# Sorted experts: the silu product kept in PSUM and split there, and the low halves of the weights shared out anew between POOL and DVE

## The reference, cut to what matters

```python
for e in range(e_tot):                                    # 9 experts, hidden width 704
    h = _silu(x_flat @ ew1[e].T) * (x_flat @ ew3[e].T)
    out = out + cw[:, e:e + 1] * (h @ ew2[e].T)            # cw: zero but for the token's two
```

## Time and profile before

| what | value |
|---|---|
| median of 3 runs | 3542.73 us |
| lowest and highest | 3534.68, 3547.43 us |
| span of the profiled execution | 3539.1 us |
| mean granted TensorE clock | 0.839 |
| busy: PE, DVE, ACT, POOL | 2583.4, 2169.0, 1432.2, 375.1 us |
| stage `m1e`: first up matmul, last down product's end | 1706.66, 1995.46 us |
| DVE cast L2058 in all: count, mean | 96, 776 ns |

### The profile page before, as it was taken

The page is one execution under the profiler, slowest core; times in us unless marked ns, Lnnn a source line. Parts: engine busy times, 40 slices in busy tenths (PEclk is TensorE's granted clock), DMA queues, the critical chain, the costliest instruction groups (busy, mean ns, idle before and its releaser), DMA issues. The chain is left out here.

```text
span 3539.1 us, 37799 instructions
## 1 busy us (share of the span) xinstructions
PE 2583.4 (73%) x12066; PEld 1640.7 (46%) x12066; DVE 2169.0 (61%) x4926; ACT 1432.2 (40%) x2245; POOL 375.1 (11%) x215
## 2 busy tenths in 40 slices
PE   2999998435566566655688458789685896899598
PEld 1444443323233333324588445556343775454387
DVE  4667666566777777743566526655663555676377
ACT  1444443111778887871333121222251231266221
POOL 0000000002000000000533302102110210200011
PEclk7999999767677777776789878989797897899699
DMA  1000000206011111000544200000430110631010
GB/s 56 14 13 14 10 13 2 83 24 195 1 25 25 25 25 25 7 1 10 177 164 161 93 27 1 0 0 0 124 79 23 42 41 14 184 87 40 28 41 30
DMA packets 72294, 170.09 MB, mean 48 GB/s; under 512 B 10184, under 2 KB 38864, under 8 KB 68688
## 3 DMA queue, kind: packets, MB, share of 16 engines
q1 hardware_dynamic: 70608, 164.11, 15.6%
q0 software_dynamic: 1536, 4.20, 0.4%
HBM read 129.09 MB, written 38.80 MB: 47 GB/s over the span
## 5 line engine op out<-in xcount | busy, mean ns | idle before, releaser
L1449 ACT ACTIVATE l1a_over_s<-l1a_sc_s,l1a_minus_step_s 128x1024 bf16<-128x1024 f32 x256 | 290.0, 1139 | 3.9 <-DVE l1a_minus_step_s L1323 2.7
L1263 DVE MAX8 l1a_cand_s<-ps 128x8 f32<-128x128 f32 x1024 | 213.2, 283 | 71.6 <-PE ps L1158 68.4
L1191 PE MATMUL ps<-l1a_probs_s,l1h_v_s 128*32 128x256 f32 x1024 | 123.9, 572 | 157.3 <-ACT l1a_probs_s L1457 156.2
L1914 PE MATMUL ps<-m1e_x_part_s,m1e_up_part_s 128*128 128x256 f32 x1152 | 170.3, 312 | 44.5 <-issue 42.8
L1435 ACT ACTIVATE l1a_sc_s<-ps,l1a_minus_tau_s 128x1024 f32<-128x1024 f32 x128 | 142.1, 1113 | 138.2 <-DVE l1a_minus_tau_s L1292 53.5
L1914 PEld LDWEIGHTS ps<-m1e_x_part_s,m1e_up_part_s 128*128 128x128 f32 x1152 | 163.1, 220 | 47.5 <-issue 45.4
L976 DVE TENSOR_REDUCE l3a_shift_s<-ps 128x1 f32<-128x1024 f32 x128 | 150.2, 1219 | 51.0 <-PE ps L893 51.0
L538 DVE TENSOR_SCALAR l0a_probs_s<-l0a_probs_s 128x1024 f32<-128x1024 f32 x128 | 88.5, 692 | 150.7 <-ACT l0a_probs_s L605 150.2
L605 ACT ACTIVATE l0a_probs_s<-ps 128x1024 f32<-128x1024 f32 x128 | 131.2, 1025 | 104.6 <-PE ps L455 103.4
L1158 PE MATMUL ps<-l1h_ka_s,l1h_qa_s 128*128 128x512 f32 x256 | 131.7, 557 | 56.6 <-DVE l1a_cand_s L1263 46.1
L1037 ACT ACTIVATE l3a_probs_s<-ps 128x512 f32<-128x512 f32 x256 | 132.8, 602 | 88.8 <-PE ps L909 88.5
(11 more groups left out here) (572 smaller groups left out, 5710.0 us busy)
## 6 DMA issues: line engine op xcount, KB each, us to landing
m1e_up_s<-m_up SPq DMA_DIRECT2D x32, 768.0 KB, 4.3
m1e_down_s<-m_down SPq DMA_DIRECT2D x16, 768.0 KB
l1h_ka_s<-l_k_parts SPq DMA_DIRECT2D x16, 512.0 KB, 7.9
l3h_ka_s<-l_k_parts SPq DMA_DIRECT2D x16, 512.0 KB, 7.9
l0a_w_s<-l_w SPq DMA_DIRECT2D x16, 384.0 KB, 3.0
m3ew_up_s<-m_up SPq DMA_DIRECT2D x6, 768.0 KB, 4.2
m_sorted<-ones SPq DMA_DIRECT2D x1, 4096.0 KB, 16.5
l1h_qa_s<-l_q_parts SPq DMA_DIRECT2D x16, 256.0 KB, 6.0
```

The lines of the kernel that those rows point to most:

```text
L1191: ins = nc.tensor.matmul(ps[32 * h:32 * h + 32, VALUES, 0:HALF], v[:, n % 2, t, h, :], probs[:, t % 4, h * HALF:(h + 1) * HALF], start=(t ...
L1263: ins = nc.vector.max(cand[:, r, 8 * (c + j * 4):8 * (c + j * 4) + 8], ps[:, A0 + f % 2, c * P:(c + 1) * P])
L1449: nc.scalar.activation(over[:, done % 2, :], sc[:, r, :], ACT.Relu, bias=minus_step[:, r:r + 1], accum_out=total[:, i, r:r + 1]).then_inc( ...
L1914: ins = nc.tensor.matmul(ps[:, u % 4, way * TOK:(way + 1) * TOK], up_parts[a][:, b % 2, k, way, c, :], x_parts[p][:, b % 2, k, :], start=( ...
```

## The change

The product of silu and up is written into the first half of the unit's own PSUM bank, over the gate values that the silu has read; high and low part are made from there, and the SBUF tile `h` is gone. DVE no longer waits for `h_ready` of two units before (there is no `h` to reuse), and PE waits for `h_ready` in place of `h_made` before it writes that bank again. `low_down` moves from DVE (after c4) to POOL (after the two up cuts of the same block). In block 0 all three low halves are made by DVE, and POOL's loop starts at block 1.

```diff
-        act_out, h = s.sb("act_out", [P, 2, TOK]), s.sb("h", [P, 2, TOK])
+        act_out = s.sb("act_out", [P, 2, TOK])
...
                 if u > 3:
-                    pe.wait_ge(h_made, u - 3)
+                    pe.wait_ge(h_ready, u - 3)
...
             def hidden(b, c):
                 u = chunks * b + c
+                h = ps[:, u % 4, 0:TOK]
                 dve.wait_ge(activated, u + 1)
-                if u > 1:
-                    dve.wait_ge(h_ready, u - 1)
-                nc.vector.tensor_tensor(h[:, u % 2, :], act_out[:, u % 2, :], ps[:, u % 4, TOK:2 * TOK], ALU.mult
-                                        ).then_inc(h_made, 1)
+                nc.vector.tensor_tensor(h, act_out[:, u % 2, :], ps[:, u % 4, TOK:2 * TOK], ALU.mult).then_inc(h_made, 1)
...
-                nc.vector.tensor_copy(h_parts[0][:, b % 2, c, :], h[:, u % 2, :]).then_inc(h_hi_ready, 1)
+                nc.vector.tensor_copy(h_parts[0][:, b % 2, c, :], h).then_inc(h_hi_ready, 1)
...
-                nc.vector.tensor_tensor(h_parts[1][:, b % 2, c, :], h[:, u % 2, :], h_parts[0][:, b % 2, c, :].bitcast(F32),
+                nc.vector.tensor_tensor(h_parts[1][:, b % 2, c, :], h, h_parts[0][:, b % 2, c, :].bitcast(F32),
...
-            def low_down(b):
-                dve.wait_ge(down_hi_ready, b + 1)
-                nc.vector.tensor_tensor(down_parts[1][:, b % 2, :, :].rearrange("p c n -> p (c n)"), down[:, :],
...
+            def first_weights():
+                for k in range(KC):
+                    dve.wait_ge(up_hi_ready, k + 1)
+                    nc.vector.tensor_tensor(up_parts[1][:, 0, k, :, :, :].rearrange("p w c n -> p (w c n)"), up[:, k, :],
...
+                dve.wait_ge(down_hi_ready, 1)
+                nc.vector.tensor_tensor(down_parts[1][:, 0, :, :].rearrange("p c n -> p (c n)"), down[:, :],
...
-            low_down(0)
+            first_weights()
             cut(0)
...
-                    if c == 4 and b + 1 < NB:
-                        low_down(b + 1)
...
+            def low_down(b):
+                pool.wait_ge(down_hi_ready, b + 1)
+                nc.gpsimd.tensor_tensor(down_parts[1][:, b % 2, :, :].rearrange("p c n -> p (c n)"), down[:, :],
...
-            for b in range(NB):
+            for b in range(1, NB):
                 for k in range(KC):
                     low_up(b, k)
+                low_down(b)
```

More of the change, by code:

```diff
@@ L2057, in hidden @@
                     dve.wait_ge(downed, b - 1)
-                nc.vector.tensor_copy(h_parts[0][:, b % 2, c, :], h[:, u % 2, :]).then_inc(h_hi_ready, 1)
+                nc.vector.tensor_copy(h_parts[0][:, b % 2, c, :], h).then_inc(h_hi_ready, 1)
                 dve.wait_ge(h_hi_ready, u + 1)
-                nc.vector.tensor_tensor(h_parts[1][:, b % 2, c, :], h[:, u % 2, :], h_parts[0][:, b % 2, c, :].bitcast(F32),
+                nc.vector.tensor_tensor(h_parts[1][:, b % 2, c, :], h, h_parts[0][:, b % 2, c, :].bitcast(F32),
                                         ALU.subtract).then_inc(h_ready, 1)
-            def low_down(b):
-                dve.wait_ge(down_hi_ready, b + 1)
-                nc.vector.tensor_tensor(down_parts[1][:, b % 2, :, :].rearrange("p c n -> p (c n)"), down[:, :],
-                                        down_parts[0][:, b % 2, :, :].rearrange("p c n -> p (c n)").bitcast(F32),
+            def first_weights():
+                for k in range(KC):
+                    dve.wait_ge(up_hi_ready, k + 1)
+                    nc.vector.tensor_tensor(up_parts[1][:, 0, k, :, :, :].rearrange("p w c n -> p (w c n)"), up[:, k, :],
+                                            up_parts[0][:, 0, k, :, :, :].rearrange("p w c n -> p (w c n)").bitcast(F32),
+                                            ALU.subtract).then_inc(up_ready, 1)
+                dve.wait_ge(down_hi_ready, 1)
+                nc.vector.tensor_tensor(down_parts[1][:, 0, :, :].rearrange("p c n -> p (c n)"), down[:, :],
+                                        down_parts[0][:, 0, :, :].rearrange("p c n -> p (c n)").bitcast(F32),
                                         ALU.subtract).then_inc(down_ready, 1)
@@ L2095, in low_up @@
                                         ALU.subtract).then_inc(up_ready, 1)
+            def low_down(b):
+                pool.wait_ge(down_hi_ready, b + 1)
+                nc.gpsimd.tensor_tensor(down_parts[1][:, b % 2, :, :].rearrange("p c n -> p (c n)"), down[:, :],
+                                        down_parts[0][:, b % 2, :, :].rearrange("p c n -> p (c n)").bitcast(F32),
+                                        ALU.subtract).then_inc(down_ready, 1)
             pool.wait_ge(places_ready, 1)
```

## The result

| what | before | changed |
|---|---|---|
| median of 4 runs each | 3539.3 us | 3489.5 us |
| lowest and highest | 3534.7, 3547.4 | 3486.2, 3491.3 |
| ratio, with its 95% interval | | 0.986 [0.984, 0.988] |
| span of the profiled execution | 3539.1 us | 3484.4 us |
| stage `m1e`, from DVE's first instruction to the last down product's end | 321.5 us | 272.2 us |

The medians differ by 49.8 us, which is 49 us by the ratio. The profiled executions differ by 54.7, but the stage by 49.2; the rest is in stages that no edit touched (4.9 us longer ahead of it, 10.4 us shorter behind it). So in what follows I compare stretches of the stage, and take medians only for the sign and size of a whole version.

What follows compares the result with a forecast made beforehand. PE was taken to wait each block for DVE's x cut, delayed by a cast held under POOL's cut. Terms -51.9 - 2.8 + 1.4 - 0.1 + 2.6 - 0.7 = -51.5 us, from 3542.7 to 3491.2 us; range 3482 to 3514.

Steps and rivals of the forecast that it cites:

- 14 blocks, with one clock loss: Blocks 1 to 14 of m1e: 14.28 us each for 251.8 in all, -51.9 us; one clock loss after block 0, +1.4.
- block 0 to 1: Wait between blocks 0 and 1: PE starts behind POOL's pair at 1720.40 instead of 1723.18, -2.8 us.
- ahead of block 0: Before the first block: x cut -0.1 us; three DVE cuts each hold one POOL scatter issue, +2.6, bounds 0 and 4.5.
- last block: The final block loses its 0.80 us wait and gets 0.1 for the slower cast: -0.7 us.
- What bounded the kernel: Between blocks PE waits 2.67 us for DVE's x cut, late because c3's cast is held until POOL's cut ends.
- The product in PSUM: DVE's unit operations, each with a PSUM operand, are no longer held; cast 0.42 us for 0.29, PSUM write also 0.42.
- The block's new length: At full clock POOL's second up cut is last: 14.28 us a block, DVE's path 13.6, PE's work 13.4 to 13.6.
- down's cut on POOL: down's low half queues behind POOL's up cuts into the next block's first 3.4 us; hidden with 1.5 us to spare.
- The rule weighed against it: Skill page rule on DVE beside descriptor generation: scatter term ahead of block 0 would be 0, sum 2.6 us lower.
- The clock rival: The clock keeps falling after each block's 0.9 us wait: 13 more losses, 18 us, giving 3509 us; chance 13%.
- The slower rival: POOL's back-to-back up and down cuts hold DVE despite PSUM operands: blocks 19.4 us, +20, 3563 us; chance 4%.

Runs made afterwards that it cites:

- e1_psum_only: The kernel before with only the silu product written to PSUM, down's low half staying on DVE: 3497.7 us, 0.988 of the kernel before.
- e2: The changed kernel with the silu product back in the SBUF tile h and its waits, weight cuts still moved: 3588.4 us, 1.014 of the kernel before.
- e4: The changed kernel with DVE's block 0 up cuts waiting for POOL's increment after its last scatter, down's cut behind the x cut: 3488.9 us, 0.986 of before.
- e5: The changed kernel with ACT making the high half of up's second half right behind the first: 3480.1 us, 0.984 of the kernel before.
- e4b_first_cuts_after_landing: The changed kernel with DVE's block 0 up cuts waiting for the scatters' own semaphore, down's cut behind the x cut: 3488.5 us, 0.987 of before.

## Why the prediction was right, point by point

3491.2 us were forecast, 3489.5 measured; a gain of 51.5 forecast, 49.2 measured in the stage. That the two times agree within 2 us is partly luck: the forecast was subtracted from 3542.7, and the kernel before had 3539.3 beside the changed one. The gain is the fairer comparison. By its steps:

| step of the prediction | forecast | measured in the stage |
|---|---|---|
| 14 blocks, with one clock loss (-51.9 + 1.4) | -50.5 | -49.6 |
| block 0 to 1 | -2.8 | -2.4 |
| ahead of block 0 (-0.1 + 2.6) | +2.5 | +3.7 |
| last block | -0.7 | -0.9 |
| sum | -51.5 | -49.2 |

- **What bounded the kernel.** "So DVE's cut of x is the last wait", late because of the held cast: shown by `e1_psum_only`, in which no cast or subtraction is held any more and all weight cuts stay where they were: it takes the block from 17.98 to 15.03.
- **The product in PSUM.** The casts' 0.42 us, taken from a row of the same shape, was measured at 0.424; the write to PSUM, for which there was no row, costs 0.012 us. Cast and subtraction were never held, in 192 of 192, 121 of which started beside a running POOL cut.
- **The block's new length.** 14.28 forecast, 14.33 measured. POOL's path is the last by 0.6 us, as laid out (1902.79 against 1902.19). The first of the blocks took 15.82, 1.5 more, for the clock loss put at 1.4. One part of the -51.9 was not named: it sets a mean block with the clock down in 12 of 14 against one at full clock. The two blocks before that kept 1.00 took 17.3 us, so about 9.5 of the 49.6 us (251.8 less 14 x 17.3, an estimate) is clock given back, and the other 40 is the wait.
- **down's cut on POOL** hidden: yes, with the 1.60 us idle ahead of POOL's next cut (the row at 1893.53) to spare, and its gain, 0.7 us a block against `e1_psum_only`, I had not priced apart.
- **Block 0 to 1.** 14.09 instead of 13.74. PE's first 48 matmuls took longer to run, and POOL's pair hangs on the second unit.
- **Ahead of block 0: the term that was mis-sized.** I took 1.0 us for each of three held issues, the middle of 0.4 and 1.6. They were held 1.31, 1.45 and 1.49, 4.25 in all, 3.83 more than before. The middle was the wrong choice: where on POOL's pitch of 1.26 a cut falls is not spread evenly. In the four executions with DVE's up cuts beside the scatters (this one, `e2`, `e4`, `e5`), the issue began 0.1 to 0.3 us into the cut in all 11 cases. Each held issue ended 0.83 us after DVE's cut did (1692.02 and 1692.85; 1694.74 and 1695.56; 1697.49 and 1698.32; in the earlier trace rows 1692.54 and 1693.37), so a hold costs what is left of the cut when the issue begins, less 0.13.
- **The rule weighed against it.** The Trainium skill, page "SBUF — State Buffer", section "Who interferes with whom", infers that a tensor_tensor and descriptor generation don't meet; by that, this term would be 0. Here each cut with two SBUF operands that ran beside the scatters held one issue, 14 of 14 in seven executions, and none took over 1.14 us where DVE did not cut. The measurement decides. Each of these issues also reads its row numbers from the SBUF tile `place_id`; whether this read or the descriptors is what is held, no run separates.
- **The clock rival** is out for this wait: with 0.69 us idle per block the clock stayed at 1.00 in 13 of 14 blocks, and the 14th came behind the 2.67 us wait of block 0. In the kernel before it was down in 12 of 14 blocks with 2.67 us, and in `e2_pool_down_sbuf_h` in all with 5.75. So the oscillation that the Trainium skill describes (page "TensorE: Matmul & The Clock Gate", section "A second HAM failure mode: psum-queue depth-cycling") was not seen with these short waits, though four PSUM banks are cycled here too.
- **The slower rival's mechanism** was right in form and is real in `e2_pool_down_sbuf_h`, where the condition holds. Its price of +20 left out the clock.

What stays open: why the untouched stages differ by 5 to 10 us between executions, and what exactly of the POOL instruction the DVE operation is held by. The runs show the condition (SBUF operands alone against one in PSUM) and the times, not the path inside. For the subtraction the operand is all that changed, its own time being 0.42 us either way. The cast also lost its faster form (0.294 to 0.424 us), and no run has a cast of the slower form that reads SBUF, so for the cast the two can't be told apart.

## What to carry to other kernels

When an engine's operation has a median of 0.3 us and a maximum of 3.3, look at what another engine was doing between its start and its end: here the 17 held casts of the kernel before each ended 0.15 to 0.16 us after POOL's cut. An operand in PSUM takes DVE out of POOL's way at 0.13 us more per cast, and only then is it worth moving more work to POOL: without it, the same moves of weight cuts made the program 1.4% slower than before. After the last wait is gone, lay out the next one from the same rows; one line moved in ACT's order was worth another 11 us in the stage.

## What was not expected of the hardware

- A semaphore increment that stands in POOL's program behind 16 indirect DMAs was done at 1688.54, when 4 of them had been issued (the fifth began at 1688.82, the last at 1705.37). It is no sign that they are through. DVE cut behind all of them once it waited for their own completion semaphore (`e4b_first_cuts_after_landing`).
- POOL's issue of an indirect DMA, 0.96 us long, is held by a DVE subtraction with two SBUF operands (1.76 us) and then takes up to 2.5 us; DVE's operation, at 1.76 us, takes no longer for it (1.75 where no issue is beside it).
- A DVE product with one operand in PSUM takes 0.428 us with its result in the same PSUM bank, 0.416 with the result in SBUF. The cast out of PSUM takes 0.424, out of SBUF 0.294.
